# One finished column closer: when GpSimd may issue the gathers of a block in a two-layer graph network

## The reference, cut to what matters

```python
# layer 0, an edge network: a 16x16 matrix per edge, made from 16 edge features
ew  = (efeat @ W_e + b_e).reshape(E, in_f, out_f)
msg = jnp.einsum('ei,eio->eo', feat[src], ew)
neigh = segment_sum(msg, dst) / max(segment_sum(ones, dst), 1)
x = _layernorm(x + neigh + bias)
# layer 1, a gated network: one of 8 matrices per edge, by its type
A = edge_emb[edge_type].reshape(-1, MSG_DIM, HID_DIM)
m = segment_sum(einsum('emh,eh->em', A, features[edge_src]), edge_dst)
# then a GRU cell of m and features, and x = _layernorm(x + h_new)
```

## Time and profile before

| | before |
|---|---|
| three executions, median | 5807.87 us |
| the profiled execution, its own time | 5833.2 us |
| its span | 5831.4 us |
| mean granted TensorE clock | 0.979 |
| TensorE matmul busy | 5227.1 us, 90% |
| VectorE busy | 4199.3 us, 72% |
| ScalarE busy | 3891.8 us, 67% |
| GpSimd busy | 3412.9 us, 59% |

### The profile page before, as it was taken

The page is one execution under the profiler, slowest core; times in us unless marked ns, Lnnn a source line. Parts: engine busy times, 40 slices in busy tenths (PEclk is TensorE's granted clock), DMA queues, the critical chain, the costliest instruction groups (busy, mean ns, idle before and its releaser), DMA issues.

```text
span 5831.4 us, 131035 instructions
## 1 busy us (share of the span) xinstructions
PE 5227.1 (90%) x41758; PEld 4693.1 (80%) x41759; DVE 4199.3 (72%) x5387; ACT 3891.8 (67%) x5533; POOL 3412.9 (59%) x3559
## 2 busy tenths in 40 slices
PE   6999999999999999999978888888888888888887
PEld 5888888888888888888767878788877788788887
DVE  7878787778777788777856666666666666666666
ACT  6666676676666666666566666666666666666664
POOL 6555565555555555555555656655655655655554
PEclk9999999999999999999989999999999999998998
DMA  3111111111111111111111111111111111111110
GB/s 66 33 30 31 33 31 31 31 31 33 30 31 33 30 31 33 31 32 31 25 23 23 23 24 23 23 23 22 23 23 23 23 23 22 24 22 23 23 23 14
DMA packets 330970, 161.25 MB, mean 28 GB/s; under 512 B 193244, under 2 KB 330011, under 8 KB 330771
## 3 DMA queue, kind: packets, MB, share of 16 engines
q1 hardware_dynamic: 218224, 130.59, 9.3%
q0 software_dynamic: 112512, 29.03, 6.3%
q10 hardware_dynamic: 160, 0.80, 0.1%
HBM read 157.44 MB, written 2.66 MB: 27 GB/s over the span
## 4 chain that ended last, share of the span: by engine, by line
PE 63%; issue 15%; DVE 12%; another core or an unknown queue 6%; DVEq 4%; ACT 0%; DMA 0%; POOL 0%; SPq 0%; ACTq 0%
PE psN L752 46%; PE psM L789 15%; DVE cand L953 6%; DVEq L997 2%; DVE nodeT L935 2%; DVE z L991 2%; DVE z L959 1%; DVEq L934 1%; DVEq L952 0%; PE psN L893 0%; PE psM L764 0%; DVEq L958 0%; PE psM L773 0%; DVE grp_hot L943 0%
## 5 line engine op out<-in xcount | busy, mean ns | idle before, releaser
L752 PE MATMUL psN<-table_hi,pick 128*128 128x320 f32 (+1 forms) x13670 | 4080.1, 316 | 167.8 <-DVE cand L953 85.3
L752 PE MATMUL psN<-table_lo,pick 128*128 128x320 f32 (+1 forms) x13670 | 3987.4, 308 | 13.7 <-issue 13.7
L752 PEld LDWEIGHTS psN<-table_hi,pick 128*128 128x128 f32 x13670 | 2598.8, 190 | 306.4 <-issue 226.1
L578 ACT ACTIVATE pick<-dist 128x640 fp32r<-128x640 bf16 (+1 forms) x2485 | 1790.5, 784 | 1336.8 <-PE psN L752 852.8
L752 PEld LDWEIGHTS psN<-table_lo,pick 128*128 128x128 f32 x13670 | 2599.6, 190 | 21.6 <-issue 21.5
L500 POOL DMA_INDIRECT z<-in_x,idx x1761 | 1704.4, 968 | 1176.9 <-issue 417.4
L500 POOL DMA_INDIRECT z<-h_rows,idx x1755 | 1682.2, 959 | 1168.3 <-issue 403.7
L570 ACT ACTIVATE dist<-src_mod,neg_node 128x640 bf16<-128x640 uint16 (+1 forms) x2485 | 1972.6, 874 | 3.3 <-DMA src_mod<-src_mod_rows 3.3
L953 DVE TENSOR_TENSOR cand<-psN,grp_hot 128x640 f32<-128x640 f32 (+1 forms) x1492 | 1122.1, 765 | 1061.3 <-PE psN L752 482.7
L991 DVE TENSOR_TENSOR z<-psD,z 128x2048 f32<-128x2048 f32 (+1 forms) x750 | 1367.8, 1824 | 55.6 <-issue 31.5
L789 PE MATMUL psM<-z,onehot 128*32 128x273 f32 (+1 forms) x12500 | 904.4, 345 | 371.4 <-issue 327.0
(11 more groups left out here) (108 smaller groups left out, 734.3 us busy)
## 6 DMA issues: line engine op xcount, KB each, us to landing
src_mod<-src_mod_rows SPq DMA_DIRECT2D x249, 192.0 KB
src_mod<-src_mod_rows SPq DMA_DIRECT2D x248, 160.0 KB
z<-in_x,idx POOLq DMA_INDIRECT x1761
z<-h_rows,idx POOLq DMA_INDIRECT x1755
eab<-in_edge_attr SPq DMA_DIRECT2D x125, 200.0 KB
idx<-in_src SPq DMA_DIRECT2D x250, 12.5 KB
dstb<-in_dst SPq DMA_DIRECT2D x250, 14.0 KB
grp<-src_grp SPq DMA_DIRECT2D x249, 5.5 KB
```

Of the source, the lines that this page charges most:

```text
L578: act.activation(pick[j][:, CHUNKS[i], 0:hi - lo], dist[i][:, 0:hi - lo], ACT.Relu, bias=1.0, scale=-1.0).then_inc(l["pick_act"], 1)
L752: mm = pe.matmul(rows[:, :, 0:cells.shape[2]], pick[j][:, c, at:at + P], cells, start=(i == 0 and part == 0), stop=(i == TC - 1 and part = ...
```

## The change

Only three tables of constants change. No instruction is added to or taken from the work itself; the waits that stand in front of the gathers change.

```diff
-AFTER_OWN = ([{5: 0, 6: 1, 7: 2, 8: 3, 12: 5, 13: 6}] * 2, [{6: 0, 7: 1, 10: 3, 11: 4, 13: 5}] * 2)
-AFTER_SUMS = (9, 8)
-AFTER_LAST = ([{0: 7, 1: 8, 2: 9, 4: 10}] * 2, [{0: 7, 1: 8, 2: 9, 4: 10}] * 2)
+AFTER_OWN = ([{4: 0, 5: 1, 6: 2, 7: 3, 8: 4, 11: 5, 12: 6}] * 2, [{4: 0, 5: 1, 6: 2, 9: 3, 10: 4, 11: 5, 12: 6}] * 2)
+AFTER_SUMS = (10, 8)
+AFTER_LAST = ([{0: 7, 1: 8, 2: 9, 3: 10}] * 2, [{0: 7, 1: 8, 2: 9, 3: 10}] * 2)
```

## The result

| | before | changed |
|---|---|---|
| median of five executions | 5802.35 us | 5847.86 us |
| span of the profiled execution | 5831.4 us | 5847.7 us |

The account below looks back on a forecast made before the run. TensorE was taken to set the pace, about a quarter of the chain not its own work. Gains 30 + 109 + 29 + 17 = 185 us, less 15, made 5833.2 into 5663, less 25 for the median: 5640 us, range 5530 to 5860.

Parts of the forecast that it names:

- the "remote" waits under 250 us: Sign: VectorE's "remote" waits at `cand` and `nodeT` fall from 576 us together to under 250.
- the pauses in layer 1: Sign: TensorE's idle time ahead of column 0 in layer 1 is gone.
- the adds within 1 us of the result's end: Sign: VectorE's adds come within 1 us of the end of TensorE's result, 3.6 us later in a layer 0 block before.
- Step 1: Gathers behind the sum, spaced out, let column 5 and the result be seen within about 0.6 us; gains 30 and 109 us.
- Step 2: VectorE's chain starts some 2 us earlier, so `z` is ready before layer 1's sum; 29 us taken of 58.
- Rival A: Pauses of 0.4 us don't count, or gathers don't cause the lateness; time as before, 5808 us; chance 0.12.
- Step 3: Around columns 7 to 4, gathers waiting for columns make layer 1's sum stalls and half clock rarer; 17 us taken of 83.
- Rival C: Layer 0's n = 8 and 9 run into the sum, costing 71 us; 5740 us; chance 0.20 with other half gains.
- Step 4: Gathers that wait later (n = 9, 12, 13, and n = 3 for VectorE's first third) delay nothing; cost 0.
- Step 5: GpSimd's own pace: three to four held waits of 1.2 us fit in a block; cost 0, bound 590 us.
- rival B: GpSimd becomes the pace with more than four held waits a block; 220 us slower, 6030 us; chance 0.16 with smaller slips.

Follow-up runs that it names:

- l0_only: The change's tables in layer 0 alone, layer 1 as in the kernel before; ratio 0.9799 to the kernel before, 5678 us.
- l1_head: Kernel before with only layer 1's gathers behind the sum changed (n = 9 to 12 wait for columns 3 to 6); ratio 1.0076.
- l1_tail: Kernel before with only layer 1's gathers ahead of the sum changed (n = 3 to 6 wait for columns 10, 0, 1, 2); ratio 0.9961.
- section 4: Its table, from traces of 14 kernels with gathers: last gather's start to the end of the sum's last stall, by the gather's place in its run.
- threes_l1: Kernel before with the changed layer 0, and layer 1's gathers gated into threes with a pause between; ratio 0.9747.
- l0_l1tail: Kernel before with the changed layer 0, and in layer 1 only the waits of l1_tail; ratio 0.9771.

## Why the prediction was wrong

The time lies inside the outer range of 5530 to 5860 us, by its slower end, but the forecast was a gain. Of the signs named for "right", the "remote" waits under 250 us and the pauses in layer 1 came true; the adds within 1 us of the result did so in layer 1 alone; layer 1's block grew instead of shrinking more than layer 0's, and its clock fell to 0.94.

**Step 1 (the run behind the sum) was right in layer 1 and wrong in layer 0.** In layer 1 pauses of 0.4 us and more do count: the result was seen 0.02 us behind its end in the mean (1.37 us before), and its pauses outside the sum fell by 1.02 us where steps 1 and 2 had 0.89 + 0.24 = 1.13. Rival A falls with it. The price was read from one block; against l0_only the pauses fell by 0.88 us. And the head itself took longer than the step had it: its six gathers started 0.3, 3.0, 4.9, 6.5, 7.9 and 9.2 us behind the sum (medians), where the forecast had 0.3, 2.0, 3.4, 5.0, 6.6 and 7.9. In layer 0 the forecast starts (0.3, 2.0, 3.7, 5.0 us) did not come about. n = 8 and 9 run at the sum's end, and n = 10 to 13 follow at once. The result is still seen 2.65 us late in the mean (3.35 before):

```profile
1179.94 0.95 POOL L500 DMA_INDIRECT z<-in_x,idx  x1 [1.11 <-remote]
...
1183.70 0.95 POOL L500 DMA_INDIRECT z<-in_x,idx  x1 [0.30 <-issue]
...
1185.93 1.13 DVE L935 TENSOR_TENSOR nodeT<-nodeT,psM 17x32 f32 x4 [2.23 <-remote]
```

Layer 0 gained all the same, and far more than the 30 us of the forecast: 2.0% in l0_only. In that kernel its sum fell to 4.59 us, from 5.18 in the profile before and 5.40 and 5.43 in l1_head and l1_tail, which have the old tables in layer 0 too. All 117 sums had a stall of over 0.5 us between two starts before, 95 of 117 there. Why the new phase of the runs suits this sum is not shown; no run changed one gate of layer 0 alone.

**Step 2 was right** as far as it went: `z` hardly held TensorE any more. But there was less to win than 58 us: the sums of layer 1 (3000 to 5760 us) waited 24.4 us for `z` before and 8.7 us after, 16 us for the 29 forecast. GpSimd's head, spread over columns, ended later and TensorE reached the sum earlier, so they met.

**Step 3 is the step that failed.** It said that a run can no longer outlive the column it waits for, and that the stalls in the sum should be rarer, worth 17 us. A gate waits for an increment that gathers hold back, so it opens 1.1 us behind the run ahead (3743.48 above), and the next run begins late, at the sum. Where the forecast had 17 us gained in all, each block of layer 1 has +1.29 us of sum and some 0.5 us of slower columns (+1.35 and 0.66 us against l0_only), or some 220 to 250 us over 123 blocks, of which the shorter pauses and layer 0 gave most back. Rival C had this mechanism with its place (gathers that run into the sum) but in layer 0; it happened in layer 1, in all blocks and not in half, and with the half clock behind it, which C did not price.

**Step 4** put n = 12 and 13 where they were, n = 13 at 7.9 us behind the sum against 7.8; it came at 9.2. It also overlooked that n = 3 to 7 shift with it: n = 7 started 20.2 us behind the last sum before and 21.1 us now, while TensorE reaches the next sum at 17.9 instead of 18.3 us (medians). Before, two gathers started in layer 1's sum; now a run of four reaches through it. **Step 5** allowed three to four held waits for nothing. In the block shown two are held, at 3738.89 and 3743.48 (0.88 and 1.12 us), and they were enough: what they cost is not GpSimd's total but where its last run stands. So rival B had the sign and the held waits, but not the place or the price (45 us for 220): TensorE was not kept waiting by `z`.

The reading behind all of this, that a run of up to three gathers hardly holds anything back, was wrong as well: by the table of section 4 a single gather holds TensorE for 1.36 us.

The rule of the Trainium skill that I set against the reading (Perfetto Trace Analysis, Per-instruction lifecycle: the update is pushed once PSUM has acknowledged, and is then propagated) names no time for either. What I drew from it, that nothing GpSimd does could hold an increment back, does not hold here: without gathers the result is seen within 0.02 us, with runs of them up to 4 us late. Which of the two steps is late no run shows.

The best version run is threes_l1, 0.9747 of the time before (5650 us), with l0_l1tail close at 0.9771. Both keep the changed layer 0.

## What to carry to other kernels

When a stall goes away on the engine that sets the pace, ask what that engine will run into next, and where the other engine's work will be by then; here 1.3 us won ahead of the sum were 1.3 us waited for in it. A gate can only delay: it fixes a phase as long as the gated engine is ahead, and once its own work delays the signal that it waits for, each gate pushes everything behind it. Test the two ends (here head and tail, or a layer) one at a time before joining them, since their effects did not add: against the layer 1 of l0_only, the tail alone took 0.10 us off a block and the head alone added 0.41, and both together added 1.12. And look at whether the profiled execution is like the others before taking a row of it as the baseline.

## What the runs showed of the hardware

- Indirect gathers on GpSimd hold back both TensorE's increments (3.35 us in the mean at layer 0's result, up to 4 us) and TensorE itself in a phase of short matmuls (five matmuls in 3.9 us). The profile gives no wait for the latter; that TensorE lacks instructions is a reading and not shown. The same GpSimd load made of memsets does neither: a mean sum of 1.65 us in layer 1.
- A single gather holds TensorE until 1.36 us behind its start; in a run with 1.26 us between starts the hold ends later with each place, 1.94 us behind the fourth's start and 2.40 us behind the seventh's. In two neighbouring blocks a run of three of which only the last reached into the sum went with a sum of 2.00 us, a run of five over it with 5.80 us.
- A sum in which TensorE was busy 1.20 of 3.20 us was followed by the 1.2 GHz level for the next columns. In layer 1 the time at that level was 0.35 us a block in l0_only, 1.24 in the profile before and 2.94 in the changed kernel.
- Leaving the gathers out, with GpSimd as busy as before, took 5787.5 - 4949.7 = 838 us off (one execution).
